# Delta-rule attention on one core: the state kept as a sum of x times delta, small-tile inverses, and a pipeline written out step by step

## The reference

```
q = x @ Wq * 128**-0.5;  k = x @ Wk;  v = x @ Wv;  beta = sigmoid(x @ Wb)
k = k * rsqrt(sum(k*k) + 1e-12)                       # for each head
S_t = S_{t-1} + k_t (beta_t * (v_t - k_t^T S_{t-1}))^T;   o_t = q_t^T S_t
o = o * rsqrt(mean(o*o) + eps) * norm_w * silu(x @ Wg)
x1 = layernorm(x + o @ Wo)
logits = x1 @ gate_w.T  -> softmax, top 2, place of each token in its expert (running count)
out = layernorm(x1 + experts(x1))
```

## Time and profile before

| | us |
|---|---|
| median of 3 timed runs | 920.72 |
| lowest and highest | 920.08, 927.41 |
| span of the profiled execution (first to last instruction) | 911.5 |
| TensorE busy in that span | 752.7 (83%) |
| VectorE, ScalarE, GpSimd busy | 419.9, 337.6, 398.9 |
| mean granted TensorE clock, share of full | 0.827 |

### The profile page before, as it was taken

The page is one execution under the profiler, slowest core; times in us unless marked ns, Lnnn a source line. Parts: engine busy times, 40 slices in busy tenths (PEclk is TensorE's granted clock), DMA queues, the critical chain, the costliest instruction groups (busy, mean ns, idle before and its releaser), DMA issues.

```text
span 911.5 us, 19015 instructions
## 1 busy us (share of the span) xinstructions
PE 752.7 (83%) x6000; PEld 653.8 (72%) x6000; DVE 419.9 (46%) x1604; ACT 337.6 (37%) x1042; POOL 398.9 (44%) x794
## 2 busy tenths in 40 slices
PE   5398988988988989989989889753999999999700
PEld 4387877877877878778778778743888888887600
DVE  3135365455455453464462653413444546566444
ACT  3235345335335334254252451212343433434200
POOL 4444565474474562654653645121242433435321
PEclk9769799779779777788785795556999999999955
DMA  7342102111111111202201111012132324524042
GB/s 281 86 136 38 36 17 50 36 35 29 35 32 31 35 34 21 43 14 40 43 14 35 23 31 35 7 54 86 60 119 79 99 89 140 156 92 144 30 121 81
DMA packets 122469, 58.46 MB, mean 64 GB/s; under 512 B 73153, under 2 KB 115521, under 8 KB 122433
## 3 DMA queue, kind: packets, MB, share of 16 engines
q1 hardware_dynamic: 117824, 48.54, 20.7%
q0 software_dynamic: 4608, 9.48, 3.1%
HBM read 30.65 MB, written 27.34 MB: 64 GB/s over the span
## 4 chain that ended last, share of the span: by engine, by line
PE 55%; DVE 18%; issue 11%; ACT 8%; POOL 3%; DMA 3%; SPq 1%; DVEq 1%; ACTq 0%; POOLq 0%
PE ps L772 8%; PE ps L782 8%; PE ps L626 6%; PE ps L513 5%; PE ps L643 4%; PE ps L651 4%; DVE A L1167 3%; DVE hb L1243 3%; PE ps L523 3%; PE ps L615 3%; ACT hs L973 3%; PE ps L561 3%; PE ps L588 2%; ACT junk L827 2%; PE ps L635 2%
## 5 line engine op out<-in xcount | busy, mean ns | idle before, releaser
L1462 POOL DMA_INDIRECT results<-ye,row x80 | 81.4, 1018 | 160.3 <-ACT ye L979 124.9
L1243 DVE TENSOR_TENSOR hb<-ps,hs 112x320 f32<-112x320 f32 x128 | 62.8, 491 | 95.4 <-ACT hs L973 92.1
L772 PE MATMUL ps<-xeTh,w13h 128*112 128x320 f32 x256 | 88.1, 344 | 9.9 <-DVE hb L1243 7.4
L1397 POOL TENSOR_TENSOR prod<-ab,xs 64x15 f32<-64x15 f32 (+7 forms) x240 | 63.8, 266 | 69.3 <-DMA ab<-a_diag 51.8
L1428 POOL DMA_INDIRECT slots_in<-x,slot x64 | 63.2, 988 | 53.4 <-DVE gates L1232 37.5
L782 PE MATMUL ps<-w2s,hb 112*128 112x128 f32 x640 | 75.5, 277 | 9.8 <-DVE hb L1243 9.8
L782 PEld LDWEIGHTS ps<-w2s,hb 112*128 112x128 f32 x640 | 72.7, 192 | 13.4 <-DVE hb L1243 8.0
L772 PE MATMUL ps<-xeTl,w13h 128*112 128x320 f32 x256 | 79.7, 311 | 0.0
L772 PE MATMUL ps<-xeTh,w13l 128*112 128x320 f32 x256 | 79.6, 311 | 0.0
L973 ACT ACTIVATE hs<-ps 112x320 f32<-112x320 f32 x128 | 56.1, 438 | 62.6 <-PE ps L772 52.5
L1398 POOL TENSOR_TENSOR xs<-xs,prod 64x15 f32<-64x15 f32 (+7 forms) x240 | 66.8, 278 | 18.8
(11 more groups left out here) (188 smaller groups left out, 1657.1 us busy)
## 6 DMA issues: line engine op xcount, KB each, us to landing
w<-w SPq DMA_DIRECT2D x32, 224.0 KB, 3.3
slots_in<-zeros SPq DMA_DIRECT2D x10, 516.0 KB, 5.4
xe<-slots_in SPq DMA_DIRECT2D x16, 322.5 KB, 3.3
results<-zeros SPq DMA_DIRECT2D x8, 512.0 KB, 5.9
yc<-results SPq DMA_DIRECT2D x32, 128.0 KB, 2.6
w2s<-w SPq DMA_DIRECT2D x16, 224.0 KB, 3.0
xTs<-xT SPq DMA_DIRECT2D x16, 128.0 KB, 3.4
a_diag<-A SPq DMA_DIRECT2D x64, 32.0 KB, 1.6
```

Of the source, the lines that this page charges most:

```text
L772: last = mm(ps[0:FW, 2 + 2 * k + g, 0:HALF], wp[:, par, k, FW * c:FW * c + FW], xp[:, par, cols], start=(t == 0), stop=(t == 2))
L1243: v.tensor_tensor(hb[:, par, c, HALF * g:HALF * g + HALF], ps[0:FW, 4 + g, 0:HALF], hs[:, g, :], ALU.mult).then_inc(h_ready, 1)
L1397: link(g.tensor_tensor(pr_, bc(ab[:, j + 1:, j], 2, j + 1), bc(xs[:, 0, j, 0:j + 1], 1, n), ALU.mult))
L1462: g.indirect_dma_start(out=y_d[b][:, :], in_=ye[:, par, i, :], in_offset=None, out_offset=bass.IndirectOffsetOnAxis(ap=row[:, par, i:i + 1 ...
```

## The change

What it does, in words. The names are those of the new kernel; p is a step, n a tile.

- The state is no longer K^T delta for each head but Z, the sum of x^T delta (128x128 for each sequence, all heads side by side). Since k = x Wk, the keys' product with the state is x (Wk Wk^T) Z. So `Wk Wk^T` and `Wq Wk^T` (128x128 for each head) are made on the chip at the start from transposed weights, `y` = (Wk Wk^T) x^T takes the place of the transposed keys, and `gq` that of the queries. Keys by token (`k_tok`) and their squares are gone. K K^T is one product of 512 columns for each sequence, x times y, and K Q^T likewise. The increment of the state is 2 products with a full stationary x and 128 columns, accumulated in PSUM over all tiles (`new_state`), in place of 8.
- The products with the state (`state_keys`) and with T (`deltas`) have the 32 columns of a head as the stationary operand and 128 columns moving; their results lie transposed, so each is followed by a copy and 2 transpositions on TensorE (`turn_keys`, `turn_deltas`).
- A is stored without its scale, and not masked. The scale c = beta over squared norm is applied to the 16x16 blocks in `scale_blocks` (VectorE), by rows, before `solve`; T carries the rest. For this the denominators of beta and the diagonal of A go through DRAM (a store and two loads more for each tile, `den_st`, `den_ld`, `ss_ld`; the store and one load move single 4-byte elements).
- The first level of the inverse uses 32 small products (32x32 stationary, 16 columns) in place of 8 full ones, and z_64, w_64 use 32x32 operands; z_128 and w_128 put the two sequences in two halves of the array. `m32`, `joins`, `x16d` and the wide part of `spread` are gone.
- The residual and the logits come out of the projection: `project` multiplies x^T by [identity, gate] and og by [Wo, Wo gate] into one bank, 136 columns, with the mean taken out of the gate beforehand. `x1_t`, `logits` and the loads of `x` for the residual are gone; x and x^T are loaded once, whole, and stay.
- Squares, the gating and the head norm's product leave GpSimd for ScalarE and VectorE.
- The running count is kept in PSUM (`count`).
- There is no loop: the steps p = -3 to 15 are written out. Step p does the first stage of tile p+3, the inverse and the query products of tile p+1, and state, output and routing of tile p. The 16x16 blocks are solved for tile p+2.

The order of a full step on TensorE is: state_keys(p), keys(p+3) first half, turn_keys(p), keys(p+3) second half, deltas(p), z_32(p+1), values(p+3), turn_deltas(p), w_32, state_queries(p), new_state(p), key_key(p+3) for sequence 0, outputs(p), z_64, key_key for sequence 1, w_64, queries(p+1) first half, head_sums(p), z_128, queries second half, w_128, gate_in(p+1), project(p), key_query(p+1) for both sequences, count(p). On ScalarE: keys_out twice, deltas_out, deltas_turned, values_out, t_diag, x64_diag, key_key_out, outputs_out, key_key_out, queries_out, head_norms, z128_copy, queries_out, t128_copy, gate_out, x1_rstd, key_norms(p+2), softmax. On GpSimd: solve(p+2), scatter(p-1), silu_of(p+1), scaled_values(p+2). VectorE's order is in the diff.

The core of the diff:

```diff
...
+def order_of_fills():
+    out = []
+    for p in range(-3, NP):
+        n1, n2 = p + 3, p + 1
+        if n1 < NP:
+            out += [("y", n1, 0), ("y", n1, 1), ("v", n1, 0), ("kk", n1, 0), ("kk", n1, 1)]
+        if 0 <= n2 < NP:
+            out += [("gq", n2, 0), ("gq", n2, 1), ("g", n2, 0), ("kq", n2, 0), ("kq", n2, 1)]
+    return out
...
+            def send_inverse(n):
+                sp.wait_ge(solved, n + 1)
+                wait(sp, xi_ld, 16 * n)
+                sp.dma_start(xi_d.rearrange("t (b r) c -> b t (r c)", r=16),
+                             xs[:].rearrange("p t r c -> p t (r c)")).then_inc(xi_st, 16)
+            def load_inverse(n):
+                sp.wait_ge(xi_st, 16 * n + 16)
+                wait(sp, w32_mm, n - 1)
+                wait(sp, xh_out, n - 1)
+                sp.dma_start(xi[:, n % 2, :, 0:16], xi_d.rearrange("t (u r) c -> r (t u) c", r=P)).then_inc(xi_ld, 16)
+            def send_blocks(n):
+                sp.wait_ge(den_out, n + 1)
+                wait(sp, den_ld, 16 * (n - 1))
+                sp.dma_start(bd_d[n % 2].rearrange("u t -> t u").unsqueeze(2), den[:, n % 2, :].unsqueeze(2),
+                             allow_slow_non_contiguous=True).then_inc(den_st, 16)
+                sp.wait_ge(a_out, 2 * n + 2)
+                wait(sp, ab_ld, 16 * n)
+                wait(sp, ss_ld, 16 * n)
+                for k in range(4):
+                    sp.dma_start(ad_d[k::4, 0:1024].rearrange("u (r c) -> r u c", c=32),
+                                 A[32 * k:32 * k + 32, n % 3, :, 32 * k:32 * k + 32]).then_inc(a_st, 16)
+            def load_blocks(n):
+                wait(sp, c2_out, n)
+                sp.wait_ge(den_st, 16 * n + 16)
+                sp.dma_start(denb[:], bd_d[n % 2].rearrange("u (k r) -> (u k) r", r=16)).then_inc(den_ld, 16)
+                sp.wait_ge(a_st, 64 * n + 64)
+                sp.dma_start(ab[:].rearrange("p (r c) -> p r c", c=16), blocks).then_inc(ab_ld, 16)
+                wait(sp, sq_out, n - 1)
+                sp.dma_start(ssd[:, n % 2, :].unsqueeze(2), diagonal, allow_slow_non_contiguous=True).then_inc(ss_ld, 16)
+            def store_x1(p):
+                sp.wait_ge(x1_ready, p + 1)
+                sp.dma_start(tile_of(x1_d, p), x1[:, p % 2, :, 0, 0:D]).then_inc(x1_st[p % 2], 16)
+            for p in range(-3, NP):
+                if 0 <= p + 2 < NP:
+                    send_inverse(p + 2)
+                if p + 3 < NP:
+                    send_blocks(p + 3)
+                if p == -2:
                     sp.wait_ge(consts_pool, 1)
                     for k in range(ROWS // P // 8):
                         sp.dma_start(xs_d[k * 8 * P:(k + 1) * 8 * P, :].rearrange("(p r) d -> p (r d)", p=P),
                                      zeros[:]).then_inc(zero_st, 16)
+                if 0 <= p + 2 < NP:
+                    load_inverse(p + 2)
+                if p + 3 < NP:
+                    load_blocks(p + 3)
+                if p == 1:
+                    for rows_d in y_d:
                         for k in range(RES // P // 8):
+                            sp.dma_start(rows_d[k * 8 * P:(k + 1) * 8 * P, :].rearrange("(p r) d -> p (r d)", p=P),
...
+            def key_key(n, b):
+                pe.wait_ge(y_free, 2 * n + 2)
+                at = free_bank("kk", n, b)
+                mm(ps[:, at, :], xTs[:, b, cols(n)], y[:, n % 3, b].rearrange("p h t -> p (h t)"),
+                   start=True, stop=True).then_inc(fill_mm, 1)
...
+            def z_32(n):
+                pe.wait_ge(xh_out, n + 1)
+                wait(pe, t128_out, n)
+                apart(pe)
                 for u in range(U):
+                    for k in range(4):
+                        s = slice(32 * k, 32 * k + 32)
+                        last = mm(ps[s, LV, 16 * u:16 * u + 16], A[s, n % 3, u, s], xh[s, n % 2, u, :],
+                                  start=True, stop=True)
+                last.then_inc(z32_mm, 1)
...
+            def state_keys(p):
+                if p:
+                    pe.wait_ge(zs_out, p)
+                    pe.wait_ge(d_out, p)
+                else:
+                    pe.wait_ge(consts_dve, 1)
+                apart(pe)
+                for b in range(B):
+                    for h in range(H):
+                        last = mm(ps[DV * h:DV * h + DV, CB, P * b:P * b + P], Zs[:, b, DV * h:DV * h + DV],
+                                  y[:, p % 3, b, h, :], start=True, stop=True)
+                last.then_inc(ks_mm, 1)
+            def turn_keys(p):
+                pe.wait_ge(ks_out, p + 1)
+                for b in range(B):
+                    last = nc.tensor.transpose(ps[:, CB, 256 + P * b:256 + P * b + P], KSt[:, b, :], ident[:])
+                last.then_inc(tr1_mm, 1)
+            def deltas(p):
+                pe.wait_ge(r_out, p + 1)
+                pe.wait_ge(t128_out, p + 1)
                 apart(pe)
                 for u in range(U):
+                    b, h = u // H, u % H
+                    last = mm(ps[DV * h:DV * h + DV, CB, P * b:P * b + P], R[:, u, :], TT[:, u, :],
                               start=True, stop=True)
+                last.then_inc(dT_mm, 1)
+            def turn_deltas(p):
+                pe.wait_ge(dT_out, p + 1)
+                for b in range(B):
+                    last = nc.tensor.transpose(ps[:, CB, 256 + P * b:256 + P * b + P], dT[:, b, :], ident[:])
+                last.then_inc(tr2_mm, 1)
...
+            def new_state(p):
+                pe.wait_ge(xk_ld[p * 2 // NP], 16 * B)
+                pe.wait_ge(d_out, p + 1)
+                if p:
+                    pe.wait_ge(slot_ready, p)
+                else:
+                    pe.wait_ge(setup_act, 2)
+                for b in range(B):
+                    last = mm(ps[:, ZA, P * b:P * b + P], xk[:, b, p, :],
+                              dl[:, H * b:H * b + H, :].rearrange("p h d -> p (h d)"),
+                              start=(p == 0 and b == 0), stop=True, skip_group_check=True)
+                last.then_inc(z_mm, 1)
-            def ks(p, par):
-                if isinstance(p, int) and p == 0:
-                    pe.wait_ge(consts_dve, 1)
-            def t_r(p):
-                pe.wait_ge(r_ready, p + 1)
-                pe.wait_ge(lvl_act, 3 * p + 3)
-                for u in range(U):
-                    last = mm(ps[:, CB, 256 + DV * u:256 + DV * u + DV], TT[:, u, :], R[:, u, :], start=True, stop=True)
-                last.then_inc(chain_mm, 1)
-            def k_d(p, par):
-                pe.wait_ge(d_ready, p + 1)
-                for u in range(U):
-                    j, h = u // H, u % H
-                    last = mm(ps[:, CB, DV * u:DV * u + DV], K[:, par, j, DK * h:DK * h + DK], dl[:, u, :],
-                              start=True, stop=True)
-                last.then_inc(chain_mm, 1)
...
+            def inverse_in(n):
+                dve.wait_ge(xi_ld, 16 * n + 16)
+                wait(dve, z32_mm, n - 1)
+                wait(dve, z64_mm, n - 1)
+                wait(dve, tdiag_out, n - 1)
+                v.tensor_scalar(x32T[:, n % 2, :, 0:16], xi[:, n % 2, U:2 * U, 0:16], low[:], None, ALU.mult)
+                v.tensor_scalar(xh[:, n % 2], xi[:, n % 2, U:2 * U, 0:16], high[:], None, ALU.mult).then_inc(xh_out, 1)
...
+            def scale_blocks(n):
+                dve.wait_ge(den_ld, 16 * n + 16)
+                dve.wait_ge(ab_ld, 16 * n + 16)
+                link(v.scalar_tensor_tensor(out=cden[:], in0=ab[:, 0:256:17], scalar=1e-12, in1=denb[:], op0=ALU.add,
+                                            op1=ALU.mult))
+                wait(dve, solved, n)
+                wait(dve, xi_st, 16 * n)
+                link(v.reciprocal(c2b[:], cden[:]))
+                v.tensor_tensor(a16[:], ab[:].rearrange("p (r c) -> p r c", c=16), bc(c2b[:], 2, 16), ALU.mult)
+                v.tensor_tensor(xs[:, 0], id16[:], bc(c2b[:], 2, 16), ALU.mult).then_inc(c2_out, 1)
...
+            def rows_of(b):
+                return ps[:, MB, XW * b:XW * b + D]
+            def normalise(p):
+                dve.wait_ge(proj_mm, p + 1)
                 for j in range(2):
+                    stats = link.mark(v.bn_stats(bst[:, j, :], rows_of(j)))
+                logits = link.mark(v.tensor_copy(lg[:], ps[:, MB, 0:2 * XW].rearrange("p (j c) -> p j c", j=2)[:, :, D:XW]))
+                link.until(stats)
+                apart(dve)
+                for j in range(2):
...
+            for p in range(-3, NP):
+                n1, n2 = p + 3, p + 1
+                first, second, main = n1 < NP, 0 <= n2 < NP, p >= 0
+                if main:
+                    keys_read(p)
+                    residues(p)
+                if second:
+                    z32_copy(n2)
+                    x32_copy(n2)
+                if main:
+                    state_copy(p)
+                if first:
+                    denominators(n1)
+                if second:
```

(64 more changed lines are left out.)

1199 lines of the change are left out of this document (558 added, 641 removed).

## The result

The kernel after takes 890.66 us (median of 4 runs, 888.64 to 891.97) against 920.92 beside it: ratio 0.964, 95% interval [0.959, 0.968]. The forecast was 823, its range ended at 888. The direction held, two thirds of the gain did not come. Executions of one kernel differ by up to 3.6% here, the longer ones mostly at a lower granted clock, so where it matters the quicker ones are compared as well as the medians.

What follows compares the result with a forecast made beforehand. TensorE bounds the kernel before; afterwards the chain through all engines ends a step. Span 73.5 + 377 + 25.7 + 25 + 26.1 + 287.2 = 814.5 us, plus 9.2 to the median: 823, range 765 to 888.

Steps and rivals of the forecast that it cites:

- the rival on 4-byte transfers: Denominators' store and diagonal's load bound the block ring; store at 15 us gives step 33, time 875; chance 0.04.
- What else could end it: Other possible bounds of a step: GpSimd's 17 us and the block ring's 19.4 us, hidden while a step is longer.
- its own ring: Solve, stores, loads and scaling of diagonal blocks; it passes 29 us once the denominators' store takes 11 us.
- signs of being wrong: TensorE without gaps; z_32 above 1.7 us; denominators' store above 5 us; first step before 65 or after 80.
- Start: Prologue up to step 0, which begins at 73.5 us; 7 to 8 us lost to clearing stores in SP's queue.
- Steps: Thirteen full steps of 29 us take 377 us; step 13 takes 25.7 and step 14 takes 25.
- The walk: Chain of one step through all engines: 16.0 us to `project`, then VectorE alone 8.7, 24.7 at full clock.
- S: Moment VectorE begins `keys_read(p)`; half clock assumed for 10.3 us from there, costing 4.6, so a step is 29.
- Full-clock rival: TensorE's clock stays up or returns at once: step 24.7 us, time 760; full clock or better overlap 0.17.
- End: Last step: 5.8 us at half clock to the state's update, then 20.3, together 26.1; experts and combining 287.2.
- Span to median: Median 920.7 lay 9.2 us above the span before; added to the forecast span 814.5, giving 823.7.
- F: Rival of the experiments, not the prediction: fetching the written-out code alone stalls the engines; time 875 to 890 in e1.

Runs made afterwards that it cites:

- e17: The kernel of e1 (denominators stored as 128 pieces of 32 bytes) run again beside e16: 802.61 us.
- e18: The kernel of e10 (denominators stored as 1024 pieces of 8 bytes) run again beside e16: 797.2 us.
- e16: The kernel after, unchanged (1024 pieces of 4 bytes), run again as the measure for three others: 872.32 us.
- e1: The kernel after with each tile's denominators stored as 128 pieces of 32 bytes instead of 1024 of 4 bytes: 791.25 us.
- e6: The edits of e1 and e4 together, with the slots' clearing stores and the loads of x moved behind the first tiles' block loads: 761.15 us.
- e7: e6 with three 512-column products a step that nobody reads, filling TensorE's wait for VectorE's tail: 723.67 us.
- e2: The kernel after without the denominators' store and load, a constant 2 in their place (output wrong): 799.68 us.
- e3: The kernel after with the 4-byte store of the denominators made twice, the second to a scratch tensor: 1002.27 us.
- e4: The kernel after with the results' clearing stores spread over steps 3 to 10 and awaited only ahead of the first send-back: 865.62 us.
- e5: The kernel after with the 4-byte store of the denominators issued from ScalarE's queue instead of SyncE's: 856.96 us.
- e9: The kernel after with only four of eight denominator columns stored, 512 pieces of 4 bytes a tile (output wrong): 919.21 us.
- e8: e6 with VectorE's copy of the state's keys and the block scaling moved ahead of placing the tile's rows: 710.87 us.
- e19: The kernel of e18 with 64 more tiny memsets at the head of VectorE's list: 815.08 us.
- e10: The kernel after with every denominator stored twice side by side, 1024 pieces of 8 bytes: 892.99 us.
- e13: The kernel of e8 with two unread 512-column products in each of the last three steps, run a second time: 749.49 us.
- e12: The kernel of e8, unchanged, run once more: 747.98 us.

## Why the prediction was wrong

**The step that failed** is in the rival on 4-byte transfers and in "What else could end it": the price of the denominators' store was taken by its number of pieces from rows with 64-byte pieces, 2.6 us and hidden. It is 11.67, and the stores of diagonal blocks behind it go from 1.6 to some 10. Written in larger pieces the same denominators cost 70 us less (e17 and e18 beside e16), about as much as the forecast was off, 67; with it mended the kernel stands at 791 to 803, below the forecast, so the other errors nearly cancel. Pieces of 8 bytes (797.2 us in e18) would have followed the rule taken from the rows; the 4-byte ones (872.32 in e16) do not. The rival that named the store, with 0.04, gave the right kind of result (33 us a step and 875; measured 31.6 and 890.66), but its number is partly luck: it needs 15 us for the store, and at the 11.67 measured its own ring gives little over 29; the rest of the 31.6 is the step of 48 us and the stalls, which it did not have. Two of the signs of being wrong came: the store above 5 us, and a first step after 80 (102.5).

Term by term, on the spans:
- *Start.* First `keys_read` at 102.5, not 73.5: 29 us. With the store mended (e1) 11 of them stay: the loads of x hold SyncE from 8.4 to 17.7, ahead of the first block store, so that the first solve begins at 29.05 and not at 23, and behind the clearing stores the next issue (`denb`, L435) takes 2.71 us by itself. Both go in e6, at 63.2.
- *Steps.* From the first `keys_read` to the last 476.7 us, not 427.7: 49. Of these some 17 are the step of 48 us, a cost that I did not have at all: I followed the clearing stores of the slots past SyncE's queue, not those of the results, nor the wait of the scatter that counts both. The other 32 are late blocks and stalls, and the clock with them: at 0.75 over these 476.7 us TensorE was at half for half of them, 238 us, where the sum had 10.3 a step, 155. The walk itself can be read in the mended kernel: in e1 the head from `keys_read` to the statistics is 19.3 us (279.31 to 298.57; 16.0 at full plus 4.6), the tail 7.4 (8.7), together 26.7 for 29.3. So the step itself was put 2.6 us too long, which hid part of the other errors. The half-clock stretch, on which the sum took 10.3 us from S on, is 281.0 to 291.3 in this step; but over the steps of e1 it is 3.5 to 14 us, so that 10.3 is one of several values. That the stretch begins at S was my estimate, and no row or run shows it as a rule: here it begins 1.7 us behind S, and the next one, at 304.9, 1.1 us ahead of its S. The 4.6 us that the sum took for it come out about right in this step, whose head is 4.4 us longer than the one at full clock in e7 (19.3 and 14.9).
- *Full-clock rival.* Its 24.7 is 22.5 in e7 (14.9 and 7.6). It did not come by itself, as forecast; here it took filler work or a shorter tail. The stretch before the fall at 261.4, against which the idle tail was held, was not without waits either: TensorE had no work for 2.7 of its 9.0 us, in waits of at most 0.88.
- *End.* 24.4 us from the last `keys_read` to the experts, 26.1 forecast; experts 286.7 for 287.2.
- *Span to median.* I added 9.2 us as what lies around the span. After, the span is 890.2 and that execution's time 891.97: 1.8 around it. The rest of the 9.2 can only be that the profiled execution before was quicker than its median. The median after is 0.5 above the profiled span, 9 less than I added. 29 + 49 - 2 - 9 = 67, which is 890.7 less 823.7.
- *Unrolling.* The sum has no term for it. That the written-out code costs nothing is not refuted and not confirmed: F alone is out, since e1 and e2 have the same written-out code and no stall.

**What stays open** is the stall without a releaser. It stood in every run with the 4-byte store (after, e3, e4, e5, e9, e16) and in none of e1, e2, e6 to e8 and e17 to e19, which ran beside e3 and e4, e5 or e16 but don't have it; that makes the store one cause. But e10 to e13 have no such store and have the stalls too, on two chips, one of which ran others without stalls before and after. In e12 the stall from 193 to 199 us falls into a stretch with DMA traffic (share 0.41 to 0.82, and none from 190 to 193); in the kernel after, the one up to 320.99 does so only in part (0.75 from 316 to 318, 0.09 up to 320, then 0.39). That the engines wait there for their own instructions, which the written-out loop has to fetch (48 packets on the instruction queue against 18 before), would fit, but no run shows it: e1 and e17 have the 48 packets too, and no stall.

## What to carry to other kernels

Price a transfer by the size of its pieces and its direction, from a row of the same size, and when no row has it, widen the range on that side instead of taking the nearest; where a layout comes down to pieces of 4 bytes, storing each number twice cost nothing that shows here and saved 75 us (872.32 in e16, 797.2 in e18). When a hand-ordered queue gains an entry, walk what stands behind it, and when a semaphore counts several groups of transfers, ask which of them the waiter needs. Where the granted clock falls at the end of each step, look for the engine whose small instructions leave TensorE idle: moving them behind the next copy gave 41 to 50 us here, filling the hole 28 to 37.

## What the hardware showed unexpectedly

- 1024 pieces of 4 bytes written: 11.67 us to landing, and the time of packets grows by 5 to 8 us of 16 engines a store (0.323 x 881.1 less 207, over 16, is 4.9 in e16; 8.2 for the second one in e3). 512 of them: 10.16 (e9). 1024 pieces of 4 bytes read: 3.0 us (`denb` in e18). 1024 of 8 bytes written: no delay that shows, the diagonal blocks behind them landed in 3.61 and 3.85 us (e18).
- The store costs others also when another engine's queue issues it (e5: diagonal blocks at 10.90 us, 38.6 us of stalls, steps of 30.5 us), while its own packets take 1.0% of the span.
- The e8 kernel ran at 711 us at one time and on one chip and at 748 on another, with 0 and 78 us of stalls, while the kernel before moved from 921.41 to 913.98. A ratio to a kernel without such stalls does not cancel them. e1 and e17 differ by 11 us, after and e16 by 18: versions are to be compared when they ran side by side.
- The 3.88 us without work at the end of a step were followed by 3.5 to 14 us at half clock, in e1's profile mostly 10 and more, in e6's mostly under 4. Filling the hole gave 28 to 37 us (e6 to e7).
